# Cross-attention pipeline of a decoder layer: a new order of each engine's work over six stages, V in one copy, the last normalisation on ACT

## The reference

```python
x = _layernorm(x + L0_attn_ref(x, ...))            # mixer
x = _layernorm(x + L0_xattn_ref(x, ctx, ...))      # cross-attention
x = _layernorm(x + L0_ffn_ref(x, ...))             # feed-forward
# cross-attention, H = 32 heads of HD = 8:
q = rope(x @ Wq);  k, v = split(ctx @ Wkv);  k = rope(k)
w = softmax(einsum('bqhd,bkhd->bhqk', q, k) / sqrt(8), axis=-1)
return einsum('bhqk,bkhd->bqhd', w, v).reshape(b, n, 256) @ Wout + bout
```

## Time and profile before

| | us |
|---|---|
| three runs | 417.89, 418.39, 422.68; median 418.39 |
| the profiled execution, its own time | 418.04 |
| its span on the page | 416.3 |
| attention steps at full TensorE clock, one | about 10.06 |

### The profile page before, as it was taken

One profiled execution on the slowest core, in us unless ns is written; L12 is line 12 of the kernel. 1 busy time (PEld: TensorE's weight loads), 2 busy tenths in 40 slices (PEclk: granted clock), 3 DMA queues, 4 the chain that ended last, 5 costly groups with the idle time before them and its releaser, 6 DMA issues.

```text
span 416.3 us, 9865 instructions
## 1 busy us (share of the span) xinstructions
PE 291.5 (70%) x3140; PEld 183.2 (44%) x3140; DVE 288.5 (69%) x643; ACT 243.7 (59%) x533; POOL 219.5 (53%) x531
## 2 busy tenths in 40 slices
PE   0361654587762656899888888888877776998872
PEld 0131533365651433544555455455444432655541
DVE  4845889978973254535777777777776338899982
ACT  4257551547652320535676666666756455799994
POOL 4301437536877853525777666667711113467674
PEclk9976585879997865556999999999999578899998
DMA  7980000000001122114233333222240000011111
GB/s 199 334 274 2 0 2 0 1 0 0 2 1 28 31 57 59 21 40 59 59 61 59 61 60 60 58 58 58 51 53 4 1 2 0 0 41 38 38 34 55
DMA packets 48819, 20.38 MB, mean 49 GB/s; under 512 B 38033, under 2 KB 47889, under 8 KB 48785
## 3 DMA queue, kind: packets, MB, share of 16 engines
q1 hardware_dynamic: 48784, 19.95, 20.6%
HBM read 9.32 MB, written 2.10 MB: 27 GB/s over the span
## 4 chain that ended last, share of the span: by engine, by line
PE 32%; DVE 16%; issue 10%; POOL 7%; ACT 5%; DVEq 1%; POOLq 0%; SPq 0%; ACTq 0%
PE psum L906 7%; DVE M L816 5%; PE psum L947 5%; PE psum L923 4%; PE psum L876 4%; PE psum L892 3%; PE psum L933 2%; ACT PO L778 2%; PE psum L1200 2%; PE psum L940 2%; DVE AT L828 2%; DVE rs L824 1%; DVE region_q L1175 1%; DVE habs L1184 1%; DVE X L1188 1%
## 5 line engine op out<-in xcount | busy, mean ns | idle before, releaser
L816 DVE TENSOR_REDUCE M<-psum 128x8 f32<-128x1024 f32 x64 | 78.0, 1219 | 35.5 <-PE psum L876 35.4
L763 ACT ACTIVATE PB<-psum,exp_scale 128x1024 f32<-128x1024 f32 x64 | 71.8, 1121 | 28.4 <-PE psum L892 27.5
L906 PE MATMUL psum<-PB,region_g 128*32 128x128 f32 x1024 | 46.1, 303 | 0.8 <-ACT PB L763 0.8
L1200 PE MATMUL psum<-FW,FXT 128*128 128x512 f16 x128 | 33.7, 411 | 7.3 <-DVE FXT L1180 5.1
L876 PE MATMUL psum<-kt,region_t 32*128 32x128 f16 x512 | 28.1, 234 | 14.2 <-DVE M L816 12.9
L876 PEld LDWEIGHTS psum<-kt,region_t 32*128 32x128 f16 x512 | 15.9, 99 | 37.0 <-DVE M L816 27.6
L906 PEld LDWEIGHTS psum<-PB,region_g 128*32 128x32 f32 x1024 | 26.5, 118 | 10.5 <-issue 4.6
L892 PE MATMUL psum<-region_t,kt 32*128 32x128 f16 x512 | 27.6, 231 | 1.3 <-ACT PB L763 0.8
L1143 ACT ACTIVATE region_q<-psum,gs 128x512 f32<-128x512 f32 x32 | 20.6, 685 | 5.4 <-PE psum L1200 5.4
L1175 DVE TENSOR_TENSOR region_q<-region_q,psum 128x512 f32<-128x512 f32 x32 | 20.8, 684 | 3.6 <-PE psum L1200 2.3
L1200 PEld LDWEIGHTS psum<-FW,FXT 128*128 128x128 f16 x128 | 12.0, 103 | 24.3 <-issue 9.5
(11 more groups left out here) (212 smaller groups left out, 819.6 us busy)
## 6 DMA issues: line engine op xcount, KB each, us to landing
X<-in_x_dram SPq DMA_DIRECT2D x4, 512.0 KB, 6.7
out_dram<-X SPq DMA_DIRECT2D x16, 128.0 KB, 1.7
region_k<-in_L_ffn_w_gate_dram SPq DMA_DIRECT2D x1, 1024.0 KB, 12.3
region_k<-in_L_ffn_w_up_dram SPq DMA_DIRECT2D x1, 1024.0 KB, 9.9
region_k<-in_L_ffn_w_down_dram SPq DMA_DIRECT2D x1, 1024.0 KB, 11.4
CS<-in_ctx_dram SPq DMA_DIRECT2D x16, 64.0 KB, 2.2
region_t<-MT SPq DMA_DIRECT2D x64, 2.0 KB
region_w<-in_L_attn_Wi_dram SPq DMA_DIRECT2D x1, 256.0 KB, 3.8
```

Source lines behind the costliest of these rows:

```text
L763: act.activation(PB[c % 2][:], ps_P, ACT.Exp, scale=exp_scale[:, 0:1]).then_inc(exp_done, 1)
L816: dve.tensor_reduce(M[:, j:j + 2, n:n + 4], ps_L, AX.X, ALU.max).then_inc(max_done, 1)
L906: ins = pe.matmul(ps_v[R * g:R * g + R, c], V[(ph - lag) % NB][:, h], PB[c % 2][:, g // 2, 2 * (g % 2) + e], start=(e == 0), stop=(e == 1) ...
L1200: ins = pe.matmul(psx[n], XT[:, c], w[c][:, half(n)], start=(c == 0), stop=(c == DC - 1))
```

## The change

1. Every engine's attention step is taken apart into small functions of one lag each and called in a new order. Logits 0 to 2 of a tile now run one step earlier (lag 1), logits 3 in lag 2, transposed logits 0 at the end of lag 2 and 1 to 3 in lag 3; the product's copy and its transposes in lag 3. POOL writes K's low half one step later than it rotates. There are six stages still.
2. V's columns of Wkv are loaded in a permuted order (eight DMAs, `load_values`, after the feed-forward weights), so that one copy of 128x256 puts V in place.
3. The last normalisation moves from DVE (L843) to ACT as scale*y + bias; POOL makes the bias (one more 128x1 instruction).
4. The drain lets three feed-forward steps stand beside steps 18 to 20 whole (FEED = 3). On PE the gate and up product of tile 0 now stands behind the whole of step 19, where before it stood inside that step. In steps 0 to 2 ACT's copy of transposed weights (L1044) stands ahead of the attention step, and PE waits for all weight copies ahead of step 2.

```diff
-        sp.dma_start(WkvS[:], Wkv).then_inc(attn_in, 16)
+        sp.dma_start(WkvS[:, 0:D], Wkv[:, 0:D]).then_inc(attn_in, 16)
...
+    def load_values(sp):
+        for a in range(2):
+            for k in range(4):
+                to = WkvS[:, D + HD * (16 * a + 4 * k):D + HD * (16 * a + 4 * k + 4)].rearrange("p (i d) -> p i d", d=HD)
+                source = Wkv[:, D + HD * 16 * a:D + HD * (16 * a + 16)].rearrange("p (i k d) -> p i k d", k=4, d=HD)
+                sp.dma_start(to, source[:, :, k]).then_inc(v_in, 16)
...
+                nc.gpsimd.tensor_tensor(rstd[:, col(t)], t1[:], K.mhalf[:, 0:1], ALU.pow).then_inc(rs2_done, 1)
+                pool.wait_ge(rs2_done, t + 1)
+                nc.gpsimd.tensor_tensor(nmr[:, col(t)], nmean[:, col(t)], rstd[:, col(t)], ALU.mult).then_inc(rstd_done, 1)
...
-                for half in range(2):
-                    act.activation(pairs[:, half, :, :, 0:HD], vs[:, half, :, :, 0], ACT.Copy)
-                    ins = act.activation(pairs[:, half, :, :, R + R // 2:R + R // 2 + HD], vs[:, half, :, :, 1], ACT.Copy)
-                ins.then_inc(V_done, 1)
+                act.activation(pairs[:, :, 0:4:3, 0:HD], ps_kv[:, D:2 * D].rearrange("p (g e d) -> p g e d", e=2, d=HD),
+                               ACT.Copy).then_inc(V_done, 1)
...
-                dve.tensor_scalar(X2[:, t5, :], Y[:, t5, :], nmean[:, col(t5)], rstd[:, col(t5)], ALU.add,
-                                  ALU.mult).then_inc(X2_done, 1)
+                act.wait_ge(rstd_done, t + 1)
+                act.activation(X2[:, t, :], Y[:, t, :], ACT.Identity, bias=nmr[:, col(t)],
+                               scale=rstd[:, col(t)]).then_inc(X2_done, 1)
```

The new order of calls on SP, on POOL and on ACT; the first number is the lag, the second the group c:

```diff
+            keys(2)
+            shifts(3)
+            context(0)
+            queries(1)
```

```diff
+            keys_low(1)
+            means(5)
+            queries(0)
+            deviation(5)
+            queries_low(0)
+            keys(0)
```

```diff
+            context(0)
+            exp(3, 1)
+            variance(5)
+            exp(3, 2)
+            keys(0)
+            values(0)
+            heads(4)
+            exp(3, 3)
+            normal(5)
+            sums(3)
+            exp(2, 0)
```

In the body of the kernel:

```diff
-        LAST_EXP = A_ALL - BESIDE + 1
+        FEED = 3
+        LAST_EXP = A_ALL - FEED
...
-                pool.wait_ge(mixer["Q_done"], NG)
                 for s in range(BESIDE, A_LOOP):
+                    pool.wait_ge(mixer["Q_done"], s // 2 + 1)
                     attn["steps"].at(att, s)
+                pool.wait_ge(mixer["Q_done"], NG)
...
                 for s in range(A_END, A_ALL):
-                    attn["steps"].at(att, s, after_exp=gate_up if s == LAST_EXP else None)
...
+                    attn["steps"].at(att, s)
+                    f = s - (A_ALL - FEED)
...
+                    if f >= 0:
+                        ffn["steps"].at(feed, f)
```

More of the change, by code:

```diff
@@ L682, in sync, with step, context, shifts @@
     def sync(sp):
[L683 to L690, removed]
+        def step(ph, *ts):
+            def context(lag):
+                t = ts[lag]
+                if t is None:
+                    return
+                i = (ph - lag) % 2
+                wait(sp, cT_done, t - 1)
+                sp.dma_start(CS[i][:], ctx_in[t]).then_inc(c_in[i], 16)
+            def shifts(lag):
+                t = ts[lag]
+                if t is None:
+                    return
+                i = (ph - lag) % NB
+                sp.wait_ge(MT_done, t + 1)
                 for j in range(4):
@@ L859, in vector, with step, context @@
+            reciprocal(4)
+            rowmax(2, 3)
+            negate(2)
+            heads(4)
+            maxima(2)
+            queries(0)
+            rowmax(1, 0)
+            rowmax(1, 1)
+            residual(4)
+            keys(0)
+            rowmax(1, 2)
         return step
     def tensor(pe):
-        def step(ph, t0, t1_, t2, t3, t4, t5, after_exp=None):
-            def logits(c):
-                if t2 is None:
+        def step(ph, *ts):
+            def context(lag):
+                t = ts[lag]
+                if t is None:
@@ L934, in step, with heads @@
                 ins.then_inc(poT_done, 1)
-            logits(3)
-            if t4 is not None:
-                pe.wait_ge(AT_done, t4 + 1)
+            def heads(lag):
+                t = ts[lag]
+                if t is None:
+                    return
+                pe.wait_ge(AT_done, t + 1)
                 at = AT[:].rearrange("p h d -> p (h d)")
@@ L948, in step @@
                 ins.then_inc(y_done, 1)
-            if t2 is not None:
-                pe.wait_ge(mn_done, t2 + 1)
-                wait(pe, MT_done, t2)
-                pe.transpose(ps_m, MN[:].rearrange("p j t -> p (j t)"), ident16[:]).then_inc(mT_done, 1)
+            context(0)
+            logits(2, 3)
+            logitsT(3, 1)
+            keys_values(0)
+            values(3, 0)
+            logitsT(3, 2)
+            maxima(2)
+            heads(4)
+            logits(1, 0)
+            values(3, 1)
+            logitsT(3, 3)
+            values(3, 2)
+            logits(1, 1)
+            output(4)
+            values(3, 3)
+            logits(1, 2)
+            logitsT(2, 0)
+            sums(3)
         return step
@@ L1457, in _ @@
                 ffn["scales"](dve, 2, 3 * B // 4, 4 * B // 4)
[L1458 removed]
+                for s in range(FEED, F_LOOP):
                     ffn["steps"].at(feed, s)
```

398 lines of the change are left out of this document (232 added, 166 removed).

## The result

| | before | after |
|---|---|---|
| runs of the first comparison, us | 417.89 to 422.68, median 418.31 | 387.34, 392.47, 398.27, 400.84, median 395.37 |
| profiled execution, its time and span | 418.04, 416.3 | 398.27, 396.2 |
| ratio after to before | | 0.930, 95% interval 0.915 to 0.945: faster |

Forecast: 403, range 386 to 418. The changed kernel's times spread over 3.4% and follow the mean granted clock of TensorE: 0.889 at 387.34, 0.880 at 392.47, 0.865 at 398.27, 0.858 at 400.84. The ratio leaves out executions more than 1.5% above the kernel's fastest, 398.27 and 400.84 here, so it can differ from the ratio of the medians.

What follows compares the result with a forecast made beforehand. Bound: the attention step's order and waits, chiefly between logits groups, then PE's clock. Up to step 6 +6.5, full-clock steps -13.9, drain -7.0: -14.4 on 418.04 gives 403.6, stated as 403; range 386 to 418.

Steps and rivals of the forecast that it cites:

- clock sooner: Rival on PE's clock: it rises in step 4, some 1.5 steps of 6.0 go, time 394; chance 0.13.
- my own case: Whole kernel, the likeliest case: 403 us, its own range 397 to 409; chance 0.50.
- Full-clock step: Attention step at full clock: 8.7 us for 10.06, between 8.45 and 10.06; gain 1.36 a step, 13.6 for ten.
- The rings I feared: Chains of dependent work in a full-clock step: variance 8.44, K's transposing DMA 8.55, beside PE's own 8.45.
- their pushing each other: Full-clock step: three rings at 8.4 to 8.6 beside PE's 8.45 may push one another, so 8.7 was taken.
- well under 35: Sign of being right: DVE's wait for logits, 35.4 us before, falls well under 35.
- Small parts: V in one copy, the normalisation on ACT and the V loads on SP: cost or give nothing.
- Start: Steps 0 to 2 get dearer: step 3 starts at 167.4, not 162.68, +4.7; bounds 0 to +8.
- I let the clock rise, as before, in the second half of step 5: Steps 4 and 5: nearly PE's work at half clock, 14.7 for 15.25, then the clock rises; together -1.3.
- Late K: Rival at PE's logits 0: K's DMA lands after 6, step 11.3, 13 steps, +33, time 436; chance 0.09.
- Drain: From step 16 to tile 1's gate and up product: 36.9 us for 43.9, -7.0, with `scales` on the path.

Runs made afterwards that it cites:

- second profile: A later profiled execution of the unaltered changed kernel: 395.34 us.
- nine profiles named above: Profiles without unread matrix products in PE's waits: six with V's copy, normalisation or K's chain altered, step 3 7.9; two unaltered and one drain-only, 12.0.
- the order alone: Changed kernel with V again in four copies and the last normalisation again on DVE, new order kept: 388.01 us, ratio 0.926.
- K a little early: Changed kernel with K's copy, rotation and high half moved slightly ahead on ACT, POOL and DVE, order of DMAs on SP kept: 393.92 us.
- K late: Changed kernel with K's high half on DVE moved behind the third maxima instead of ahead of them: 425.25 us, ratio 1.006.
- logits joined: Changed kernel with logits group 0 issued later on PE, so that groups 0 and 1 touch: 416.58 us, ratio 0.987.

## Why the prediction was right, and where it was off

The range and the direction held: 395 of four executions (392.6 of all ten) for 403, in 386 to 418. The measured median is nearer to the rival "clock sooner" (394) than to my own case (397 to 409), and in the profiled execution two large misses of opposite sign partly cancel. So the bound of the full-clock step was understood; that 403 is not further off is in part luck.

- **Full-clock step: 8.7 forecast, 8.52 measured.** PE's own work is the bound now, as said, and joining two groups brings 10.09 back. The reading of what bound it before was too narrow: I took the waits between groups of logits for PE's whole 1.6 us; they were 0.6 of it, and the waits for the product's copy and for the division, the other 1.0, went with them. The rings I feared do stand just under PE: POOL ends K's rotation at 278.38 (277.66 + 0.72) and DVE takes it at 278.42; K lands 0.3 to 0.4 ahead of PE's question. My 0.2 for their pushing each other was too much. DVE's wait for logits fell only from 35.4 to 29.5 and not "well under 35". In steps 6 to 15 it went from 14.5 to 12.5, with 9.8 of the rest in steps 3 to 5: DVE still has idle time and takes it there. The better witness is PE's wait for maxima in those ten steps, 5.9 before and 1.4 after.
- **Small parts: nothing forecast, nothing measured in the time.** The normalisation on ACT takes 0.63, more than the 0.4 to 0.55 I put, and hides. That one copy of V holds ACT for about as long as four was wrong: 0.26 to the next instruction, not 0.42. By the figures of the Trainium skill ("ScalarE: Activation LUTs", What ACT_TABLE_LOAD costs) I had an estimate of some 0.6 for the four; three kernels show 0.42.
- **Start: +4.7 forecast, +3.8 measured** (+2.0 in the second profile), step 3 12.1 forecast, 12.0 measured in both. The way was the one described: the mixer's transposes start at 150.26, where I had put 151.
- **"I let the clock rise, as before, in the second half of step 5": this step failed.** It rose in the middle of step 4, and steps 4 and 5 took 19.8 for the 26.4 that follow from the forecast: 6.6 us, the largest miss. In six of the nine profiles named above it was even back by the start of step 3. This is the rival "clock sooner", which I held at 0.13. The rule beside it (the Trainium skill, "TensorE: Matmul & The Clock Gate", A second HAM failure mode: psum-queue depth-cycling) pointed the right way: with one pause between groups back in every step the clock rose at 193, with the pauses of steps 1 and 2 filled at 163. These traces agree with it but don't prove it, since six kernels with those pauses unfilled had the clock back at 163 to 164 as well.
- **Late K: held at 0.09 as a state of every step, and it came in two.** Steps 6 to 15 took 90.3, where ten of 8.7 are 87: 5.1 us of late K and half clock against 1.8 of shorter steps. (In the second profile K was late too, 1.11 us in step 10, the clock held, and the ten steps took 87.6.) The rival put the turn to slower at a step of 9.9; with one instruction moved the full-clock step was 9.8 and the median 425. Its mechanism was right; its price left out the clock, which took the steps at changing clock to 11.9.
- **Drain: 36.9 forecast, 36.5 measured**, and `scales` stood on the path as said. That the two agree to 0.4 is luck: the second profile, with more time at half clock, has 39.9.

Made up for the profiled execution: start 0.9, steps 3 to 5 6.7, steps 6 to 15 -3.3, drain 0.4, rest of the span 1.0 sooner than forecast, together 5.7; 403.6 less 5.7 is 397.9, for 398.27.

## What to carry to other kernels

Four dependent groups that share two banks want other work of the length of the consumer between them, and not one bare gap: here a single one gave back the whole gain of the full-clock step. Before naming one ring as the bound, list what the bounding engine itself waits for in one step: here it waited for three things. When an order is packed until PE is the bound, read the spare time of every transfer that PE asks for; here 0.3 to 0.4 us was left, and losing it cost more than the wait wherever the clock fell too. Step 3 took 12.0 us at half clock and 7.9 at full clock, so keeping PE busy in the first steps is worth trying. And look at more than one profile: the same kernel's drain took 36.5 and 39.9.

## What the runs showed of the hardware

**K's late landings stand beside fetches of instructions.** Its DMA lands after 3.0 to 3.3 us in most steps. The DMA view of three such transfers in the changed kernel, at 206.4, 223.5 and 232.5, shows each time one packet of an instruction queue beside them; they land after 3.1, 3.8 and 4.7. In the stretch 262.5 to 266.2 there is none and the landing is 3.1. The views from 223.5 to 226.8 and from 232.5 to 235.9:

```profile
q1 hardware_dynamic: 1739, 0.43, 96.4%
q14 instruction: 1, 0.01, 0.6%
...
kt<-KA SPq DMA_TRANSPOSE x1, 3.8
```

```profile
q1 hardware_dynamic: 1952, 0.48, 75.2%
q8 instruction: 1, 0.02, 1.7%
...
kt<-KA SPq DMA_TRANSPOSE x1, 4.7
```

Over 56 such transfers in four profiles (the changed kernel twice, the order alone, K a little early; K's DMAs from the third on), 27 had an instruction packet within 3.3 us of their start: median landing 3.6, up to 5.0. The other 29 had a median of 3.1. All ten landings of 3.9 or more are among the 27; the lowest of the 27 is 3.1, so a packet does not always cost. In six more profiles of the new order 13 such transfers took 3.9 or more, 12 of them beside a packet. The kernel before had two, 4.9 (from 190.58) and 4.4 (from 304.11), each beside a q8 packet, and PE never waited for K there: it is the slack that the new order changed, not the landing. In every kernel of the new order but those with K late or the logits joined, the longest wait for K or Q from step 3 on stands in step 10, whether that step began at 222 or at 233: it goes with a place in the program, not with the time. From about 252 to 288 of the changed kernel's profile, in the loop's second turn, no packet is seen, and there the steps are 8.42 to 8.53 without a break. The Trainium skill ("Runtime: NRT & Kernel Launch", Instruction fetch mechanics) says that each sequencer refills in blocks of 16 KiB over a DMA queue of its own and that this is mostly hidden; that size agrees with the q8 packet's 0.02 MB, not with the q14 packet's 0.01. If the fetch is what delays K, then it is not hidden here, as K has hardly any slack. That it is the cause is not shown: the two coincide in time, however regularly, and no run took the fetches away or moved them.

**The clock at the edge.** After the wait of step 10 the clock fell where that was 1.15, 1.29, 1.31, 1.35, 1.44 or 1.66 us; it held after 0.97, 1.11 (twice) and 1.18 (twice). But in the kernel with K late it held after 1.26, 1.27, 1.30 and 1.31 in the last steps. So one wait's length does not settle it, and what else does stays open.
